# Four graph layers on one core: logits at the end of the tiled matmuls, gate bias as a 32-partition tile beside them, V copied by VectorE, gate bias split in small pieces, first weight splits later

## The reference

```python
h = maximum(layernorm(x), 0); x = x + L0(h, adj)   # attention, 6 heads of 64
h = maximum(layernorm(x), 0); x = x + L1(h, adj)   # graph attention with gate, 12 heads of 32
h = maximum(layernorm(x), 0); x = x + L2(h, adj)   # as L0, other weights
h = maximum(layernorm(x), 0); x = x + L3(h, adj)   # as L1, other weights

# L0, L2
q, k, v = heads(h@Wq+bq), heads(h@Wk+bk), heads(h@Wv+bv)
probs = softmax(q k^T / 8 + where(adj, 0, -9e15))
out = (probs v) @ Wf + bf

# L1, L3
g = einsum('bnd,ade->bane', h, W);  th = tanh(g)
attn = leaky_relu(th w_src + (th w_dst)^T, 0.2)
attn = softmax(where(adj, attn, -999))
f = elu(attn g + b)
gate = sigmoid(h @ H_w.T + H_b)
out = gate * f + (1 - gate) * h
```

## Time and profile before

| | |
|---|---|
| median of 3 runs | 2066.66 us (2066.53 to 2067.69) |
| profiled execution | 2066.47 us |
| its span | 2064.7 us |
| instructions | 58618 |
| TensorE matmul busy | 97%, weight loads 90% |
| ACT / DVE / POOL busy | 95% / 89% / 76% |
| granted TensorE clock, mean | 0.988 |
| DMA | 130.64 MB, 63 GB/s |

### The profile page before, as it was taken

How to read it: one execution, slowest core, us unless ns; L and a number is a source line. 1 busy time by engine, 2 the same in 40 slices (tenths; PEclk the granted TensorE clock), 3 DMA queues, 4 the chain that set the end, 5 groups by cost and what they waited for, 6 DMA issues and landing times.

```text
span 2064.7 us, 58618 instructions
## 1 busy us (share of the span) xinstructions
PE 1997.0 (97%) x19596; PEld 1848.1 (90%) x19596; DVE 1841.5 (89%) x4117; ACT 1958.6 (95%) x6800; POOL 1569.5 (76%) x2874
## 2 busy tenths in 40 slices
PE   6899999999999999999999999999999999999973
PEld 6899999999999999999999999999999999999962
DVE  5589999999999999999999999999999999999875
ACT  4699999999999999999999999999999999999985
POOL 5568888788887777777777777777777777777764
PEclk9999999999999999999999999999999999999997
DMA  5012222323322222223332221222212212212112
GB/s 161 16 41 64 72 72 74 78 70 83 87 68 72 55 57 53 53 56 97 99 102 53 53 56 52 56 53 54 59 49 53 58 49 56 58 49 52 41 40 62
DMA packets 309219, 130.64 MB, mean 63 GB/s; under 512 B 229430, under 2 KB 308668, under 8 KB 308924
## 3 DMA queue, kind: packets, MB, share of 16 engines
q1 hardware_dynamic: 308924, 126.90, 23.7%
HBM read 69.42 MB, written 57.41 MB: 61 GB/s over the span
## 4 chain that ended last, share of the span: by engine, by line
PE 64%; ACT 21%; DVE 9%; issue 4%; POOL 2%; DMA 1%; SPq 0%; POOLq 0%; DVEq 0%; ACTq 0%
PE psum L744 27%; PE psum L754 13%; ACT LG L515 10%; ACT LA L509 5%; DVE LG L635 4%; DVE neg_max L639 4%; PE psum L831 3%; PE psum L842 3%; PE psum L853 3%; PE psum L736 3%; PE psum L819 3%; PE psum L771 2%; PE psum L871 2%; PE psum L776 2%; ACT PTA L581 1%
## 5 line engine op out<-in xcount | busy, mean ns | idle before, releaser
L515 ACT ACTIVATE LG<-LG,neg_max 128x128 f32<-128x128 f32 x1536 | 595.9, 392 | 28.1 <-DVE neg_max L639 26.9
L509 ACT ACTIVATE LA<-LA,neg_max 128x128 f32<-128x128 f32 x768 | 299.2, 410 | 0.0
L515 ACT ACTIVATION_READ_ACCUMULATOR LG<-LG,neg_max 128x1 f32 x1536 | 293.2, 191 | 0.0
L427 POOL TENSOR_TENSOR prod<-th,vec 128x384 f32<-128x384 f32 x256 | 256.1, 1023 | 21.3 <-ACT th L556 20.9
L635 DVE COPY_PREDICATED_SCALAR LG<-no_edge,no_edge_score 128x1536 f32 x128 | 254.2, 1986 | 4.5 <-ACT LG L547 4.5
L639 DVE TENSOR_REDUCE neg_max<-LG 128x12 f32<-128x1536 f32 x128 | 224.4, 1753 | 14.1 <-DVE LG L635 0.5
L423 POOL TENSOR_TENSOR ey<-ey,hG 128x384 f32<-128x384 f32 x128 | 131.7, 1029 | 113.7 <-ACT ey L550 113.7
L407 POOL TENSOR_SCALAR ey<-y 128x384 f32<-128x384 f32 x128 | 65.0, 507 | 193.2 <-DVE y L687 193.2
L754 PE MATMUL psum<-hT_hi,qk_lo 128*128 128x256 f32 x1152 | 200.0, 281 | 0.0
L754 PE MATMUL psum<-hT_lo,qk_hi 128*128 128x256 f32 x1152 | 199.3, 282 | 0.0
L754 PE MATMUL psum<-hT_hi,qk_hi 128*128 128x256 f32 x1152 | 199.2, 281 | 0.0
(11 more groups left out here) (125 smaller groups left out, 6234.0 us busy)
## 6 DMA issues: line engine op xcount, KB each, us to landing
context<-gcT SPq DMA_DIRECT2D x512, 48.0 KB, 2.1
back<-context SPq DMA_DIRECT2D x128, 192.0 KB, 2.4
xin<-x SPq DMA_DIRECT2D x64, 192.0 KB, 2.6
x_mid<-x SPq DMA_DIRECT2D x64, 192.0 KB, 1.9
xin<-x_mid SPq DMA_DIRECT2D x64, 192.0 KB, 2.6
out<-x SPq DMA_DIRECT2D x64, 192.0 KB, 1.9
ahead<-stage SPq DMA_DIRECT2D x16, 288.0 KB, 3.1
stage<-w_vf SPq DMA_DIRECT2D x8, 288.0 KB, 4.0
```

Of the source, the lines that this page charges most:

```text
L427: last = pool.tensor_tensor(prod[:, i, :], th[:], vec[:, r.pair(k - 2), 2 + i, :], ALU.mult)
L509: last = act.activation(head, head, ACT.Exp, scale=-1.0, bias=neg_max[:, 0, h:h + 1], accum_out=rsum[:, h:h + 1])
L515: last = act.activation(head, head, ACT.Exp, bias=neg_max[:, 1, a:a + 1], accum_out=den[:, a:a + 1])
```

## The change

- All five engines get a new order of their blocks and new offsets; the steps run from -7 to 133 instead of -5 to 134. On PE: h (k-1), graph context (k-3), attention context (k+1), V (k+3), Q/K pieces 1 and 0 (k+5), O (k+1), Q/K piece 2, probability transposes, sdT (k-1), more of them, hM (k+7), hG (k), attention probability transposes (k+2), the last probability transposes (k-2), scores (k+3), logits (k-1), gate with its bias (k).
- The logits come right behind the scores. The gate bias follows the logits as a matmul of 32 partitions (96 to 127), and the nine gate matmuls follow it.
- V is copied from PSUM by VectorE instead of ScalarE.
- The splits of H_b are made for both pairs at once on 24 partitions x 32, in five operations at step -3; the three parts go to HBM and come back as three partitions of hb3.
- The pieces of the weights are split in another order (Q and K first, then V, O, gate, h), at the steps -6 to -2 (low parts) behind the first blocks of VectorE's step, high parts at -7 to -3.
- Both output biases are made at the steps -3 and -2. PSUM banks are given out anew.

```diff
-FIRST_STEP, STEPS_BEHIND = -5, 7
+FIRST_STEP, STEPS_BEHIND = -7, 6
+        hb_parts = nc.dram_tensor("hb_parts", (PARTS, PAIRS * D), BF16, kind="Internal").ap()
-        SPLIT_STEPS = {-4: range(0, 3), -3: range(3, 6), -2: range(6, 8), -1: range(8, 11), 0: range(11, 14)}
+        SPLIT_STEPS = {-6: range(0, 3), -5: range(3, 6), -4: range(6, 8), -3: range(8, 11), -2: range(11, 14)}
+        HIGH_STEPS = {-7: range(0, 3), -5: range(3, 8), -4: range(8, 11), -3: range(11, 14)}
...
SP
-                sp.dma_start(hb_row[:, pair, :], h_b[pair].partition_broadcast(PARTS)).then_inc(s["hb_in"], 16)
+            sp.dma_start(hb_row[:], h_b.rearrange("k (a e) -> (k a) e", e=GD)).then_inc(s["hb_in"], 16)
+                if k == -2:
+                    sp.wait_ge(s["hb_step"], 5)
+                    sp.dma_start(hb_parts.rearrange("p (a e) -> a p e", e=GD), hb_part[:]).then_inc(s["hb_out"], 16)
+                if k == -1:
+                    sp.wait_ge(s["hb_out"], 16)
+                    sp.dma_start(hb3[ROWS:ROWS + PARTS, :, :].rearrange("p k n -> p (k n)"), hb_parts).then_inc(s["hb_back"], 16)
...
POOL, the new order of a step: layernorm m (k+5), x1+hG (k-4), neg_bias (k+1), prod (k-3), ey-hG (k-6),
hM (k+5), score_parts (k-3), no_edge (k-2), split_ahead, layernorm g (k-1), xin+bias (k), y+x1 (k-6),
y_min (k-5), sigmoid (k-3)
+            def head_bias():
+                part = [hb_part[:, p, :] for p in range(PARTS)]
+                pool.tensor_copy(part[0], hb_row[:]).then_inc(s["hb_step"], 1)
+                pool.wait_ge(s["hb_step"], 1)
+                pool.tensor_tensor(hb_rest[:], hb_row[:], part[0], ALU.subtract).then_inc(s["hb_step"], 1)
+                pool.wait_ge(s["hb_step"], 2)
+                pool.tensor_copy(part[1], hb_rest[:]).then_inc(s["hb_step"], 1)
+                pool.wait_ge(s["hb_step"], 3)
+                pool.tensor_tensor(hb_row[:], hb_rest[:], part[1], ALU.subtract).then_inc(s["hb_step"], 1)
+                pool.wait_ge(s["hb_step"], 4)
+                pool.tensor_copy(part[2], hb_row[:]).then_inc(s["hb_step"], 1)
...
+                if k == -3:
+                    pool.wait_ge(s["hb_in"], 16)
+                    head_bias()
...
ACT, the new order of a step: sdT (k-2), PTG 1 (k-3), hT_hi (k+6), gT_hi (k-1), PTA (k+1), hG (k), leaky (k-2),
PTG 2 (k-3), Q/K 2, exps (k+2), th (k-1), ey (k-4), gate (k-1), cT_hi (k+1), graph exps 4-7 and 0-3 (k-2),
Q/K 1 and 0, graph exps 8-11 (k-2), PTG 0 (k-2)
-                    act.wait_ge(s["m_v"], r.done(k + 3))
-                    act.activation(v[:, (k + 3) % 4, :], bank(3)[:, 0:D], ACT.Copy).then_inc(s["m_val"], 1)
...
DVE, the new order of a step: row maxima (k+1), y (k-5), statistics of xin (k+7), split_low, mask and maxima (k-3),
gcT (k-4), hv (k-2), cT_lo (k), sd (k-2), rden and LA (k+1), elu and mix (k-5), V, x1 and statistics (k), sdR (k-2),
hT_lo (k+6), gT_lo (k-1), rdenG (k-3)
+                if r.has(k + 2):
+                    dve.wait_ge(s["m_v"], r.done(k + 2))
+                    dve.tensor_copy(v[:, (k + 2) % 4, :], bank(3)[:, 0:D]).then_inc(s["m_val"], 1)
...
PE, the end of a step
+                if r.has(k - 1):
+                    pe.wait_ge(s["g_sdR"], r.done(k - 1))
+                    wait_latest(pe, r, ("m_lo", k + 7), ("qk0", k + 5), ("z_leaky", k - 2))
+                    wait_latest(pe, r, ("pt", k + 2), ("gpt0", k - 2), ("cT_lo", k + 1), ("z_leaky", k - 2))
+                    for q in range(QUADS):
+                        rows = slice(q * GROUP, (q + 1) * GROUP)
+                        last = pe.matmul(bank(1 + q), sdT[rows, (k - 1) % 2, :], sdR[rows, (k - 1) % 2, :, :].rearrange("p a n -> p (a n)"), start=True, stop=True)
+                    last.then_inc(s["z_ps"], 1)
+                if r.has(k):
+                    weights("gate", k)
+                    pe.wait_ge(s["g_lo"], r.done(k))
+                    wait_latest(pe, r, ("g_lo", k), ("qk1", k + 5), ("g_gate", k - 1))
+                    pe.matmul(bank(0)[:, 0:D], ones[ROWS:128, :], hb3[ROWS:128, r.pair(k), :], start=True, stop=False)
+                    nodes_times(bank(0)[:, 0:D], g_hi, g_lo, hg_hi, hg_lo, D, begun=True).then_inc(s["g_gate_ps"], 1)
...
             def setup(k):
-                for pair, at in ((0, -1), (1, 1)):
+                for pair, at in ((0, -3), (1, -2)):
```

More of the change, by code:

```diff
@@ L342, in straight @@
                                  ).then_inc(stored[slot], 16)
[L343 to L347, removed]
+            for k in range(-3, ALL + 6):
                 straight(k)
@@ L393, in step @@
             def step(r, k):
[L394 to L402, removed]
+                if r.has(k + 5):
+                    layernorm(r, "m", 0, k + 5)
@@ new lines, in step @@
+                if r.has(k - 3):
+                    pool.wait_ge(s["g_th"], r.done(k - 3))
+                    for i in range(2):
+                        last = pool.tensor_tensor(prod[:, i, :], th[:], vec[:, r.pair(k - 3), 2 + i, :], ALU.mult)
+                    last.then_inc(s["g_prod"], 1)
+                if r.has(k - 6):
+                    pool.wait_ge(s["y_exp"], r.done(k - 6))
+                    pool.tensor_tensor(ey[:], ey[:], hG[:, (k - 6) % HELD, :], ALU.subtract).then_inc(s["ey_f"], 1)
@@ L778, in step @@
-                if r.has(k - 3):
-                    pe.wait_ge(s["g_sdR"], r.done(k - 3))
-                    wait_latest(pe, r, ("gpt1", k - 4), ("pt", k), ("z_leaky", k - 4))
-                    wait_latest(pe, r, ("s_max", k + 1), ("qk2", k + 2), ("z_leaky", k - 4))
-                    wait_latest(pe, r, ("g_sdR", k - 3), ("s_max", k + 1), ("qk1", k + 2), ("z_leaky", k - 4))
-                    for q in range(QUADS):
-                        rows = slice(q * GROUP, (q + 1) * GROUP)
-                        last = pe.matmul(bank(4 + q), sdT[rows, (k - 3) % 2, :], sdR[rows, (k - 3) % 2, :, :].rearrange("p a n -> p (a n)"), start=True, stop=True)
-                    last.then_inc(s["z_ps"], 1)
@@ new lines, in step @@
+                if r.has(k - 2):
+                    pe.wait_ge(s["z_exp0"], r.done(k - 2))
+                    wait_latest(pe, r, ("cT_lo", k + 1), ("z_leaky", k - 2), ("pt", k + 1), ("gpt0", k - 3))
+                    for a in range(0, 4):
+                        last = pe.transpose(bank(2)[:, (a % 4) * N:(a % 4 + 1) * N], LG[:, a * N:(a + 1) * N], idf[:])
+                    last.then_inc(s["gpt_ps0"], 1)
+                if r.has(k - 1):
+                    pe.wait_ge(s["g_sd3"], r.done(k - 1))
+                    wait_latest(pe, r, ("s_max", k + 2), ("g_sdR", k - 2))
```

559 lines of the change are left out of this document (262 added, 297 removed).

## The result

The changed kernel takes 2051.44 us (median of 4 runs, 2050.59 to 2052.94) against 2066.77 beside it: a ratio of 0.9926, 95% interval 0.9911 to 0.9941, so 15.3 us faster. The forecast was 2035, 31.7 us faster. The sign and the range hold; the size is half of what was forecast, and the step of the working that failed has to be found.

The account below looks back on a forecast made before the run. The prediction took PE's instruction stream as the bound: 88.9 fill + 1805 (118 steps of 15.30) + 29.9 + 80 + 29.9 = 2034 us span, + 1.8 = 2035.5, forecast 2035; own range 2018 to 2046, whole range 2014 to 2066.

Parts of the forecast that it names:

- Is PE still the limit?: Steady step: with V's copy on DVE, ACT 14.72 and DVE 14.84 us in 15.30, so PE still sets the step.
- the tightest round: Steady-step circle through DVE and POOL, from scores ready to PE's next scores: 14.8 us, 0.5 under PE.
- Rival 1: Steady step: a DVE or POOL wait partly replaces PE's limit, step 15.40, 12 us more, 2047; chance 0.15.
- So a steady step lasts as long as PE's instruction stream: Plateau of the kernel before: PE busy throughout, no PE wait for another engine, so PE's stream sets the 15.44 us step.
- the first term, the bias: PE's gate bias as a fourth row tile beside the logits: gain 0.07 us per step.
- The second, 0.07 for the entry at the logits: PE's logits follow the already tiled scores and lose their own entry; 0.01 back at h: gain 0.07 us per step.
- the lower bound 15.22: Shortest steady PE step allowed, with some 0.05 us of small hM wait going too; the upper bound was 15.61.
- rival 3: Steady step and fill: bias columns behind logits, entry back, step 15.45, fill as long as before; 2062 us; chance 0.09.
- PE being the limit, neither end moves my sum: Steady step: port sharing gives DVE up to 0.5 us back or makes POOL's short operations wait; neither changes the forecast.
- Fill: Start-up: small gate bias splits and earlier q and k; first full step starts at 88.9 us instead of about 98.1.
- Drain: End of run: 80 us (70 to 88) from after step 122 to the last logits, then 29.9 to the end.
- Rival 2: Steady step: the DVE-POOL round becomes the limit above the old step, 15.8 us, 2094 in all; chance 0.14.

Follow-up runs that it names:

- the two V runs: V's copy put back on ACT in the changed kernel: 2049.23 us; V's copy moved to DVE in the kernel before: 2064.51 us.
- the last POOL run: Changed kernel with POOL's score parts ahead of hM and the gate bias as one 128-partition matmul behind the logits: 2044.88 us, ratio 0.9896.

## Why the prediction was wrong

Its sum against the changed kernel's own execution (span 2048.5, forecast 2034):

| term | forecast | measured | difference |
|---|---|---|---|
| first full step starts | 88.9 | 93.4 | +4.5 |
| 118 full steps | 15.30 each | 15.41 each | +12.9 |
| steps 121 and 122 | 29.9 | 30.0 | +0.1 |
| from there to the last logits | 80 | 77.5 | -2.5 |
| last logits to the end | 29.9 | 29.3 | -0.6 |

**The step that failed is "Is PE still the limit?".** It summed the tightest round to 14.8 us, 0.5 under PE, and concluded "All close, none late". The real round was 0.1 over PE, and it alone makes 12.9 of the 14.4 us by which the sum is short. That sum followed sd down DVE's queue, to the probabilities and back through sdR, and left out the branch on POOL: behind the products stand ey - hG (1.03), hM (0.67) and the five score-part operations, and PE's transposes wait for these. With them the round is 15.40, and without hM in front it is below 15.29. Rival 1, a DVE or POOL wait at a step of 15.40 and 2047, named the size; its place, DVE with V's copy, was wrong, as the two V runs show. It had 0.15. The same step took DVE at 14.84 us of a step, 194 of 200; it was 186.25, for the two-input passes came out shorter (the probabilities' 1285 ns in the mean instead of 1458), so DVE's load was never what was close.

**PE's 15.30 came true by luck.** The forecast took 0.14 from 15.44. Once POOL is out of the way the same matmuls run at 15.29. But the 15.44 was not PE's stream: "So a steady step lasts as long as PE's instruction stream" was wrong for the kernel before, whose stream is 15.36 and whose step the round of ACT and DVE holds. So the stream lost 0.07, and that is the first term, the bias. The second, 0.07 for the entry at the logits, is not there. The changed order with the bias in its old form runs at 15.36 too (the last POOL run), as the kernel before does. The start was 0.08 too high, the saving 0.07 too large, and the two cancel. In the parts: scores to gate is 1.19 (1001.35 to 1002.54) as forecast; h ahead of the graph contexts takes 1.66 (1004.21 to 1005.87) against 1.59, so 0.07, where I took 0.01. The Trainium skill, "TensorEngine Tiling (Array Packing)", Key Properties, says that a change of tiling mode drains the engine; by the prediction's count of such changes no entry is won and the gain per step is the bias's 0.07. The trace agrees with that count, with 15.36 and 15.29.

Two smaller sums do not close either: the lower bound 15.22 is not reached by the 0.05 that it names (15.25), and rival 3 by its own terms (0.16 for the bias's columns, 0.07 for the entry) is a step of 15.53 and not 15.45.

**"PE being the limit, neither end moves my sum" was the second error in that step.** The prediction weighed what happens when a DVE pass with two SBUF inputs meets POOL's short operations, and set it aside since PE was the limit. The first cast of the score parts, in the changed kernel and in the one with POOL reordered (ns min/median/max):

```profile
L389 POOL CAST sd<-sd x128: 202/922/952, 70.7 to 2015.1; 128x24 bf16<-128x24 f32 x128
```

```profile
L389 POOL CAST sd<-sd x128: 204/204/558, 70.2 to 2003.2; 128x24 bf16<-128x24 f32 x128
```

The same 24 elements take 922 or 204 ns. In the changed kernel DVE's probabilities' pass, issued while hM runs, is 1.32 long, and the cast ends with it (1012.60 and 1012.54); in the other the pass takes 0.96 and it is the subtraction (L391, 0.84) that ends with it (1249.56, 1249.46). The Trainium skill, "SBUF — State Buffer", section on the two separate sides, has the pair of ports held for a whole instruction by whoever starts first; the trace agrees in both directions. In the changed kernel the parts take 2.58 us, in the kernel before some 2.0 (five operations with their gaps). Those 0.5 alone would have made the round shorter than PE; but no run took the meeting away, since the reordering leaves the parts at 2.50 and takes away hM's place. What is shown is hM's place; that the ports would have done as well is argued.

**Fill.** The mechanism was right: `head_bias` was the hole, and without it PE is busy. The first full step starts 4.5 late. By step the forecast is met at the end of step -4 (25.6 and 25.63); 4.0 of the difference arise in the next three (step 0 starts at 53.50, forecast 49.5). PE's timeline:

```profile
23.04 0.63 PE L747 MATMUL psum<-hT_hi,qk_hi 128*128 128x256 f32 x3 [0.47 <-DVE hT_lo L672]
...
25.63 2.10 PE L882 MATMUL psum<-LG 128*128 128x384 f32 x6
27.27 0.98 PE L737 MATMUL psum<-vf_hi,hT_hi 128*128 128x384 f32 x3
...
33.66 2.20 PE L882 MATMUL psum<-PTG 128*128 128x384 f32 x6
35.41 0.98 PE L737 MATMUL psum<-vf_hi,hT_hi 128*128 128x384 f32 x3
...
41.04 0.52 PE L729 MATMUL psum<-idf,hM 128*128 128x128 f32 x3 [0.38 <-ACT QKT L517]
42.01 0.84 PE L837 MATMUL psum<-idf,LA 128*128 128x128 f32 x6 [0.45 <-DVE v L656]
```

Each output bias is 1.64 or 1.75 us where I took 0.8: plain fp32, not the split form, and so 6 records for 3 matmuls. That is 1.8 of the 4.5, and the two listed waits for ACT and DVE are 0.8; the other 1.9 are not placed (1.4 in these three steps, 0.5 behind them). POOL's `head_bias` went as estimated:

```profile
16.46 0.44 POOL L450 CAST hb_part<-hb_row 24x32 bf16<-24x32 f32 x1 [6.79 <-DMA hb_row<-h_b]
...
18.26 0.20 POOL L458 CAST hb_part<-hb_row 24x32 bf16<-24x32 f32 x1
```

h_b landed at 16.5 (18 forecast), the five operations took 2.0 (1 to 2.5), and PE, which runs q and k from 15.57 on, loses at most the 0.47 at 23.04 by it (1 forecast). **Drain** was right within 3 us, on the good side. Rival 2 (2094) and rival 3 (2062) did not come.

## What to carry to other kernels

A PE that is busy for all of a window is not proof that PE sets the step: both kernels here showed 200.00 of 200 us busy, with waits of 0.08 and 0.11 us in each step. Read the chain over the whole run and not in one window: it gave ACT 21% and DVE 9% of the span in the kernel before, and POOL 10% in the changed one. Compare the spacing of one and the same group at two places (0.50 here, 0.45 there) and of the whole step early and late (15.36, 15.44), or take work out of the engine and see if time falls. If it does not, look on the other engines for the operation that ends just ahead of a PE instruction, and ask what stands in front of it in its queue that is needed later; sum every branch of a round, not the first that looks tight. Two engines that each wait for the other in every step, however shortly, are a sign of a round between them.

## What the runs showed of the hardware

- A POOL cast of 128 x 24 took 204 ns or 922 ns, by whether it met a two-input DVE pass; that pass took 0.96 us or 1.32, by whether it met a POOL operation. The order of two POOL operations thus sets both.
- A 32-partition matmul with 384 columns beside three with 512 cost PE nothing: from the logits to the gate's first matmul are 0.32 us with it and 0.32 without. (The times, 2051.4 and 2049.4, cannot tell it alone, for POOL's wait hid the 128-partition form in the same kernel.) As 128 partitions behind them it cost 0.07 a step (15.36 against 15.29), 6.8 us in all, but only where PE was the limit.
- Four fp32 transposes took 0.44 to 0.45 us ahead of other transposes, 0.53 ahead of the 32-partition logits (before) and 0.53 ahead of the 64-partition scores (after). The price of this entry moved with the new order and was not saved.
